# Macaron block on one Trainium2 core: the second feed-forward layer as seven half products, with values and keys staged through DRAM by group and by half

## The reference

```python
def ffn(x):                      # k0: 512 x 1024, k1: 1024 x 1024, k2: 1024 x 256, entries +1 or -1
    h = concatenate([x, -x], axis=-1)
    h = relu(s0 * (h @ k0)) * 2
    h = relu(s1 * (h @ k1)) * 2
    return s2 * (h @ k2)
x = x + 0.5 * ffn(layernorm(x))
x = x + attention(layernorm(x))  # q, k, v projections with biases, softmax, output projection
x = x + 0.5 * ffn(layernorm(x))
```

## Time and profile before

| | us |
|---|---|
| median of 3 runs | 1525.29 |
| span of the profiled execution | 1521.2 |
| TensorE busy | 1512.4 |
| ScalarE busy | 1129.3 |
| VectorE busy | 574.2 |
| GpSimd busy | 59.7 |

### The profile page before, as it was taken

How to read it: one execution, slowest core, us unless ns; L and a number is a source line. 1 busy time by engine, 2 the same in 40 slices (tenths; PEclk the granted TensorE clock), 3 DMA queues, 4 the chain that set the end, 5 groups by cost and what they waited for, 6 DMA issues and landing times.

```text
span 1521.2 us, 31574 instructions
## 1 busy us (share of the span) xinstructions
PE 1512.4 (99%) x12471; PEld 606.1 (40%) x12471; DVE 574.2 (38%) x1298; ACT 1129.3 (74%) x1654; POOL 59.7 (4%) x65
## 2 busy tenths in 40 slices
PE   9999999999999999999999999999999999999999
PEld 5555455334334333333333334334333334334354
DVE  7645764511431243234332333242241332323462
ACT  3221222888889988898989989889988988988721
POOL 2010011001000100010100000000000000000000
PEclk9999999999999999999999999999999999999999
DMA  4122223212331231232223123111213212311110
GB/s 139 42 84 51 75 80 113 71 51 81 84 73 41 96 95 40 67 113 63 81 53 95 40 53 94 39 49 59 81 39 67 82 51 65 104 41 21 47 28 16
DMA packets 110139, 101.46 MB, mean 67 GB/s; under 512 B 55846, under 2 KB 95526, under 8 KB 109990
## 3 DMA queue, kind: packets, MB, share of 16 engines
q1 hardware_dynamic: 109158, 98.60, 23.0%
q10 hardware_dynamic: 832, 0.79, 0.2%
HBM read 61.87 MB, written 25.43 MB: 57 GB/s over the span
## 4 chain that ended last, share of the span: by engine, by line
PE 99%; DVE 0%; ACT 0%; issue 0%; POOL 0%; POOLq 0%
PE psum L888 31%; PE psum L850 30%; PE psum L872 16%; PE psum L750 12%; PE psum L762 3%; PE psum L738 3%; PE psum L769 2%; PE psum L782 1%; PE psum L688 0%; PE psum L775 0%; DVE xn L972 0%; DVE h_lo L982 0%; PE psum L710 0%; DVE x_sb L987 0%; ACT xn L911 0%
## 5 line engine op out<-in xcount | busy, mean ns | idle before, releaser
L942 ACT ACTIVATE prob<-psum 128x512 f32<-128x512 f32 (+1 forms) x1438 | 1016.6, 784 | 120.1 <-PE psum L872 115.4
L888 PE MATMUL psum<-prob,v_sb 128*17 128x512 f32 x4096 | 489.4, 595 | 0.0
L872 PE MATMUL psum<-q_st,k_st 64*128 64x512 f16 x2048 | 350.1, 379 | 0.2
L915 ACT ACTIVATE h_hi<-psum 128x512 f16<-128x512 f32 x183 | 109.6, 604 | 215.8 <-PE psum L750 164.6
L980 DVE TENSOR_SCALAR h_hi<-psum 128x512 f16<-128x512 f32 x73 | 50.5, 692 | 433.8 <-PE psum L850 433.8
L982 DVE SCALAR_TENSOR_TENSOR h_lo<-psum,h_hi 128x512 f16<-128x512 f32 x256 | 169.0, 688 | 86.9 <-ACT h_hi L915 84.4
L888 PEld LDWEIGHTS psum<-prob,v_sb 128*17 128x17 f32 x4096 | 95.3, 96 | 262.9 <-issue 166.4
L872 PEld LDWEIGHTS psum<-q_st,k_st 64*128 64x128 f16 x2048 | 82.5, 94 | 279.1 <-ACT prob L942 210.7
L850 PE MATMUL psum<-h_hi,w 64*128 64x512 f16 x1184 | 152.1, 376 | 0.2 <-ACT h_hi L915 0.2
L850 PE MATMUL psum<-h_lo,w 64*128 64x512 f16 x1184 | 152.0, 376 | 0.0
L750 PE MATMUL psum<-h_hi,w 128*128 128x512 f16 x432 | 102.5, 380 | 2.2 <-DVE h_lo L982 2.2
(11 more groups left out here) (109 smaller groups left out, 860.0 us busy)
## 6 DMA issues: line engine op xcount, KB each, us to landing
k_st<-k_halves SPq DMA_DIRECT2D x64, 512.0 KB, 4.4
q_halves<-piece SPq DMA_DIRECT2D x32, 256.0 KB, 2.5
q_st<-q_halves SPq DMA_DIRECT2D x64, 128.0 KB, 4.8
x_rows<-x_sb SPq DMA_DIRECT2D x16, 256.0 KB, 2.2
k_halves<-piece SPq DMA_DIRECT2D x16, 256.0 KB, 2.8
att_rows<-o_sb SPq DMA_DIRECT2D x128, 32.0 KB
x_sb<-x_rows SPq DMA_DIRECT2D x8, 512.0 KB, 4.0
att_t<-att_rows SPq DMA_DIRECT2D x16, 256.0 KB
```

What stands on the lines that cost most here:

```text
L872: mm = pe.matmul(psum[:, score_bank[h + r], :], k_st[rows, slot, t * P:(t + 1) * P], q_st[rows, slot, :], start=True, stop=True)
L888: mm = pe.matmul(psum[32 * j:32 * j + va, O_BANK, :], v_sb[:, b * key_tiles + t, GROUP * g4 + j, :], prob[:, h % PROBS, :], start=(t == 0) ...
L915: act.activation(hi, psum[:, bank, :], ACT.Relu).then_inc(act_done, 1)
L942: act.activation(prob[:, to:to + count, :], psum[:, bank:bank + count, :], ACT.Exp, scale=score_scale / QK_SCALE ** 2).then_inc(exp_sem, 1)
```

## The change

The second layer of every block but block 0 is computed by Strassen's algorithm in the form with 7 products and shared sums. The 1024 x 1024 weights are cut in 2 x 2 quarters, the activations in 2 x 2 by features and by tokens (256 tokens, `HALF`). Each product is a quarter of the weights, or a sum of quarters, by a quarter of the activations or a sum of them; it is laid in two halves of 256 output features ("p" steps: 14 a block), each 16 matmuls of 128 rows and 256 columns (high and low parts, 4 contraction tiles, 2 output tiles). The two tiles share a bank ahead of and behind attention. Products 2, 7, 4 and 3 go on in the bank of the product before them (`BEFORE`), once that has been read; product 4 adds to 7, which adds to 6.

- **Weights:** `w1` holds the quarters and three sums made by GpSimd; the fourth sum takes the place of a quarter behind block 0's second layer ("w3").
- **Operands:** the first layer's output goes as float32 to `sums` (one buffer, 8 slots, used also for the products). Per pair of tiles VectorE makes T1 to T4, then their high and low parts in float16 (4 x 256 elements); ScalarE, or VectorE in the attention stage, makes the high parts of the three plain quarters and GpSimd their low parts (3 x 256 elements).
- **Outputs:** VectorE adds every product to a sum; products 2, 4, 5 and 3 give a rectified quarter of the result each, high part by ScalarE (VectorE in the attention stage) and low part by VectorE ("low").
- **Order:** "norm" is split in "stat" and "norm"; the normalized rows are GpSimd's but for the first. The first layer of the next block stands ahead of or between the third layer's fills. The attention stage begins with the first layer of block 5. In it a product is one step of 16 slots of 256 columns (two banks, 256 columns of each), a third layer has 13 slots a step for 16, and both rectifications of a first-layer pair are VectorE's.
- **Staging:** values go to DRAM (`v_rows`) by block; for each group values and keys are fetched in two halves of eight key tiles into a single buffer each, in steps 5 and 1 of a group, after the half that they replace has been read. Queries are fetched as before.
- Scaling constants of the first layer are halved (`ACT0_SCALE`).

The core of the diff:

```diff
+A11, A12, A22, S1, S2, S3, S4 = range(7)
+A21 = S3
+B11, B21, B22, T1, T2, T3, T4 = range(7)
+PRODUCTS = {
+    1: (A11, B11, True, None, (1, 0), (0, 1)),
+    2: (A12, B21, False, 0, (2, 0), (0, 2)),
+    6: (S2, T2, True, None, (0, 1), (0, 1)),
+    7: (S3, T3, False, None, (0, 1), (0, 1)),
+    4: (A22, T4, False, 2, (1, 1), (0, 2)),
+    5: (S1, T1, True, 3, (1, 1), (0, 2)),
+    3: (S4, B22, False, 1, (1, 1), (0, 2)),
+}
+FIRST_OF = {1: 1, 2: 1, 6: 6, 7: 6, 4: 6, 5: 5, 3: 5}
+BEFORE = {2: 1, 7: 6, 4: 7, 3: 5}
+OF_QUARTER = {0: 2, 1: 3, 2: 4, 3: 5}
...
-        steps = [Step("norm", u, kind), Step("xn", u, kind)]
+        steps = [Step("stat", u, kind), Step("norm", u, kind), Step("xn", u, kind)]
         if kind == 1 or u:
             steps += [Step("split", u, kind), Step("flip", u, kind)]
         return steps
+
+    def products(u):
+
+        if u <= qblocks or u >= 2 * blocks - 1:
+            order = ((1,), (6,), (2,), (7, -2), (5,), (4, -5), (3, -4, -3))
+        else:
+            order = ((1,), (2, -2), (6,), (7,), (4, -4), (5, -5), (3, -3))
+        return [[Step("p" if k > 0 else "low", u, 8 * half + abs(k)) for k in ks]
+                for half in range(2) for ks in order]
...
+        for i, product in enumerate(second):
+            if i == 3 and ahead is not None and ahead < blocks:
                 steps += norm_turn(0, ahead)
...
+            if early and i == 7:
                 steps += projections(behind)
...
+            if project and i == (11 if last else 9):
                 steps += project + norm_turn(2, ahead)
...
+            if last and i in (0, 2):
+                steps += divide[2 * i:2 * i + tpb]
+            steps += product
+            if not last and i in (2, 5):
+                steps += divide[tpb * (i // 3):tpb * (i // 3 + 1)]
...
+        if ahead is None:
+            steps += third_layer(u)
+        elif last:
+            steps += third_layer(u) + first_layer(ahead)
+        elif u < qblocks:
+            steps += first_layer(ahead, (0, 1)) + third_layer(u, (0,)) + first_layer(ahead, (2,))
+            if behind is None:
+                steps += first_layer(ahead, (3,)) + third_layer(u, (1,))
+            else:
+                steps += third_layer(u, (1,)) + first_layer(ahead, (3,))
+        else:
+            steps += first_layer(ahead) + third_layer(u)
...
-    PAIRS = {"l1": (4, 4), "l2": (5, 3), "l3": (10, 6), "qk": (1, 1), "v": (2, 2), "out": (2, 2)}
...
+    PAIRS = {"l1": (4, 4), "p": (8, 8), "l3": (8, 5), "qk": (1, 1), "v": (2, 2), "out": (2, 2)}
...
+    LONG = {"stat": 0.45, "norm": 0.6, "xn": 0.05, "split": 0.4, "flip": 0.6, "merge": 0.4, "heads": 0.26, "peak": 0.3}
...
+        lay_long(0.6 if side[0].kind == "p" else math.inf)
...
+    while in_group():
+        lay_pair(side[0].n - side[0].hi if side[0].kind == "p" and side[0].n else 16 if side[0].kind == "p" else 64)
+        lay_idle(att_steps)
+        lay_long(math.inf)
...
-        v_sb = sb("v_sb", [P, tokens // P, heads, va], F32)
+        v_new = sb("v_new", [P, block_groups, tpb, GROUP * va], F32)
+        v_st = sb("v_st", [P, key_tiles, GROUP * va], F32)
...
-        w1 = sb("w1", [P, kh, hidden], F16)
+        w1 = sb("w1", [P, 7, kh // 2, hidden // 2], F16)
...
+        h0_hi = sb("h0_hi", [P, 7, kh // 2, HALF], F16)
+        h0_lo = sb("h0_lo", [P, 7, kh // 2, HALF], F16)
...
-        k_st = sb("k_st", [P, 4, seq], F16)
+        k_st = sb("k_st", [P, 2, seq], F16)
+        sums = sb("sums", [P, 8, HALF], F32)
...
+            pool.tensor_tensor(w1[:, S1], w1[:, A21], w1[:, A22], ALU.add).then_inc(w1_sums, 1)
+            pool.wait_ge(w1_sums, 1)
+            pool.tensor_tensor(w1[:, S2], w1[:, S1], w1[:, A11], ALU.subtract).then_inc(w1_sums, 1)
+            pool.wait_ge(w1_sums, 2)
+            pool.tensor_tensor(w1[:, S4], w1[:, A12], w1[:, S2], ALU.subtract).then_inc(w1_sums, 1)
...
+                    if j == 0 and product in BEFORE:
+                        before = find["p", u, 8 * half + BEFORE[product]]
+                        wait_held(before)
+                    if half == 0 and tile == 0:
+                        wait_operand(u, product, low, k)
+                    mm = pe.matmul(psum[:, bank, tile * HALF:(tile + 1) * HALF],
+                                   w1[:, weights, k, (2 * half + tile) * P:(2 * half + tile + 1) * P],
+                                   (h0_hi, h0_lo)[low][:, operand, k, :], start=(starts and j == 0), stop=(j == s.n - 1),
+                                   skip_group_check=True)
...
+                for tile in range(2):
+                    r = (tile + turned) % 2
+                    rows = slice(64 * r, 64 * r + 64)
+                    mm = pe.matmul(psum[:, SHARED[tile], 0:HALF],
+                                   w1[rows, weights, k, (2 * half + tile) * P:(2 * half + tile + 1) * P],
+                                   (h0_hi, h0_lo)[low][rows, operand, k, :], start=(starts and i == 0), stop=(i == s.n - 1),
+                                   skip_group_check=True)
...
+        def sums_free(engine, s):
+
+            u, j = s.u, s.m % 4
+            if j or sums_no[u]:
+                engine.wait_ge(low_b, kh // 2 * sums_no[u] + j)
+            if j:
+                engine.wait_ge(dve_done, find["l1", u, j - 1 + kh // 2].dve)
+            elif sums_no[u]:
+                for product in (2, 5, 4, 3):
+                    engine.wait_ge(dve_done, find["low", sums_of[sums_no[u] - 1], 8 + product].dve)
...
+        def act_first(s):
+
+            u, m = s.u, s.m
+            act.wait_ge(mm_done, s.mm)
+            if m < kh // 2:
+                sums_free(act, s)
+            act.activation(b_rows(sums, m), halves_of(psum[:, s.bank, :]), ACT.Relu).then_inc(act_done, 1)
+            if m >= kh // 2:
+                act.wait_ge(act_done, s.act0 + 1)
+                act.wait_ge(mm_done, last_product(u).mm)
+                act.activation(h0_hi[:, 0:3, m % 4, :], sums[:, 0:3, :], ACT.Copy).then_inc(act_done, 1)
+
...
+            dve.tensor_tensor(sums[:, T1, :], sums[:, T1, :], sums[:, B11, :], ALU.subtract).then_inc(dve_done, 1)
+            dve.wait_ge(dve_done, at + 1)
+            dve.tensor_tensor(sums[:, T2, :], sums[:, B22, :], sums[:, T1, :], ALU.subtract).then_inc(dve_done, 1)
+            dve.wait_ge(dve_done, at + 2)
+            dve.tensor_tensor(sums[:, T3, :], sums[:, T2, :], sums[:, B11, :], ALU.subtract).then_inc(dve_done, 1)
+            dve.tensor_tensor(sums[:, T4, :], sums[:, B21, :], sums[:, T2, :], ALU.subtract).then_inc(dve_done, 1)
+            dve.wait_ge(dve_done, at + 4)
+            dve.wait_ge(mm_done, last_product(u).mm)
+            dve.tensor_copy(h0_hi[:, 3:7, j, :], sums[:, 3:7, :]).then_inc(dve_done, 1)
+            dve.wait_ge(dve_done, at + 5)
+            dve.tensor_tensor(h0_lo[:, 3:7, j, :], sums[:, 3:7, :], h0_hi[:, 3:7, j, :], ALU.subtract).then_inc(dve_done, 1)
+
...
+                dve.tensor_tensor(sum_of(product), both, sum_of(to), ALU.add).then_inc(dve_done, 1)
+            if not s.on_act and PRODUCTS[product][3] is not None:
+                dve.wait_ge(dve_done, s.dve0 + 1)
+                dve.tensor_scalar(second_pair(h1_hi, s.m), sum_of(product), 0.0, None, ALU.max).then_inc(dve_done, 1)
...
+            dve.scalar_tensor_tensor(second_pair(h1_lo, s.m), sum_of(s.m % 8), 0.0, second_pair(h1_hi, s.m),
+                                     ALU.max, ALU.subtract).then_inc(dve_done, 1)
...
-                dve.tensor_scalar(xn[:, place[u, s.m], t, :], x_sb[:, u % RING, t, :], moment[:, n % 2, t, 0:1],
+                engine.tensor_scalar(xn[:, place[u, s.m], t, :], x_sb[:, u % RING, t, :], moment[:, n % 2, t, 0:1],
                                   rstd[:, n % 2, t:t + 1], ALU.subtract, ALU.mult).then_inc(ln_x, 1)
...
+                elif s.kind == "l1" and u and m >= kh // 2 and s.last():
+                    if s.on_act:
+                        pool.wait_ge(act_done, s.act)
+                    else:
+                        pool.wait_ge(dve_done, s.dve0 + 2)
+                    pool.tensor_tensor(h0_lo[:, 0:3, m % 4, :], sums[:, 0:3, :], h0_hi[:, 0:3, m % 4, :], ALU.subtract
+                                       ).then_inc(low_b, 1)
+                elif s.kind == "xn" and norm_no[u, m]:
+                    normed(pool, s)
...
+                    g, step = divmod(s.u, group_steps)
+                    if step == 0 and g + 1 < groups:
+                        sp_stage_q(g + 1)
+                    if step == 1 and g:
+                        sp_stage_keys(g, 1)
+                    if step == group_steps // 2 + 1 and g + 1 < groups:
+                        sp_stage_keys(g + 1, 0)
...
+            if g:
+                sp.wait_ge(qk_sem, 2 * key_tiles * (g - 1) + (half + 1) * key_tiles)
+                sp.wait_ge(pv_sem, key_tiles * (g - 1) + (half + 1) * key_tiles // 2)
...
+                sp.dma_start(k_st[:, pair, at], k_rows.unsqueeze(1).broadcast_to((4 * hd, 2, seq // 2))
```

(4 more changed lines are left out.)

467 lines of the change are left out of this document (340 added, 127 removed).

## The result

The changed kernel takes 1737.85 us (median of 4 runs, 1736.32 to 1739.76) against 1524.8 (1523.85 to 1525.33): ratio 1.14, 95% interval 1.1384 to 1.1416. The forecast was 1664, the top of its range 1698: the direction was right, the time 74 us too short and outside the range. The profiled execution's span is 1735.8 us.

The account below looks back on a forecast made before the run. VectorE's queue, stretched by GpSimd, was to become the bound at every first layer. TensorE's 1467.6 + 32 + 37 + 71 + 42 + 10 = 1660, + 4.1 = 1664 us; range 1548 to 1698.

Parts of the forecast that it names:

- TensorE's own account: Whole kernel: TensorE's own work falls from 1521.2 to 1467.6 us (less 11.4, 14.0, 16.5, 11.7) if no queue falls behind.
- the waits before products 7 and 4: Ahead of attention, blocks 1 to 4: TensorE waits for VectorE's reads behind normalizations, 3.4 and 4.6 us, 32 in all.
- the first layer's waits ahead of attention: First-layer pairs of 6.6 us, single buffer of sums: TensorE waits 12 before block 1, 8.2 in blocks 2 to 4; 37.
- The normalized rows on GpSimd: Each normalization: rows moved from VectorE (1.38 us) to GpSimd, taken as 1.45 us, with VectorE waiting for them.
- the upper bound of 2.4: Normalized rows on GpSimd: at most 4 x 256 x 2.31 ns = 2.4 us, from its two-input rows.
- six gaps: Lower granted clock behind TensorE's gaps, 1.7 us each: one in blocks 1 to 4 each, two behind attention; 10 us.
- Attention's pairs, 71: In attention a first-layer pair takes VectorE 7.28 us in steps of 4.56: TensorE loses 7.1 in each of ten blocks.
- Exclusion: First-layer pairs: GpSimd's subtraction cannot run beside VectorE's two-input sums, so a pair takes 6.6 us, not 4.96; forecast case, 0.62.
- side by side: Rival: VectorE and GpSimd overlap at first-layer pairs, so their waits shrink and the time is 1580 us; chance 0.26.
- The forecast's weighing of the earlier trace: A 64-element VectorE sum took 1.69 us beside GpSimd's 1024-element addition; taken as exclusion, though possibly a one-partition oddity.
- Behind attention, 42: Waits behind attention: product 4 12.7 us behind reciprocals, product 3 7.5, block 15's first layer 18, same-bank products 4.
- Staging: Three more transfers a group on SP's queue, priced at nothing; rival that halves land late: up to 146 more, chance 0.03.

Follow-up runs that it names:

- the extra matmuls: Changed kernel plus 22 matmuls at each of eight waits before products 7 and 4: behind the bank's wait 1751.45 us; ahead of every wait 1733.65 us.
- the memset: Changed kernel with GpSimd's subtraction of 768 elements replaced by a memset to zero, low parts left out: 1665.63 us, ratio 1.0928.

## Why the prediction was right in direction and 74 us short

By stage, the forecast against the span: ahead of attention 225.6 of own work + 69 of waits + 6.8 of clock = 301.4, measured 330.2; attention 1151.7 + 71 = 1222.7, measured 1264.0; behind it 72.1 + 42 + 3.4 = 117.5, measured 123.4. The differences, 28.8 + 41.3 + 5.9, make up the 76 between 1660 and 1735.8. By term, the forecast was too low by 51 for the clock, 18 for TensorE's own account, 18 for the waits before products 7 and 4 and 1 for all other waits, and too high by 12 for the first layer's waits ahead of attention.

**"The normalized rows on GpSimd: [...] I take 1.45, as it is a one-input operation"** failed: 4.83, twice the upper bound of 2.4. The bound was worked out from two-input rows on the belief that one input is cheaper. For an operation with two constants that holds, in a row of the kernel before that the forecast does not show:

```profile
L617 POOL TENSOR_SCALAR wq_sb<-wq_sb 128x512 f32<-128x512 f32 x1 | 0.6, 620 | 0.1
```

That is 1.2 ns an element. The normalized rows take two scalars per partition (mean and reciprocal root) in place of constants and took 1.22 us for 256 elements, 4.8 ns each. No row of the kernel before had this form on GpSimd, so the bound was none. Eight waits before products 7 and 4 sum to 49.9 for 32. The forecast's working with 4.83 in it gives 59, so part of this error was covered by luck: the working overrates these waits. Put back on VectorE the rows give 35.9 us, close to half of the 74, some 11 of it through the clock.

**The clock: "I charge six gaps [...]: 10. In attention the bound is ten more, 17; I take 0"** failed, and this is the largest term. Busy time over the own work is 29.9 ahead of attention and 8.7 behind it, and 22.3 in attention against the same matmuls at 1.00: 61 us. The price of one gap was near (1.7 forecast, 2.3 seen behind a wait of 6.9); the count was not. The changed kernel's trace has 27 stretches at the lower level, 12 ahead of attention (three a block), 12 in it and 3 behind it, 2.3 us each. In attention the waits recur 27 times at the pairs, and the scores between them did not keep the clock up; with the memset, where the waits at the pairs fall from 49.6 to 26.6, two stretches are left there. The 61 are not all time, as the extra matmuls show: ahead of attention part of them lies between two waits for VectorE.

**The first layer's waits ahead of attention** were 24.8 where I had 37: 9.5 before block 1 for 12, and about 5 in each of blocks 2 to 4 for 8.2. A pair takes 6.34 there and not 6.6, which gives 1 us a block; the rest is open. The clock is not the reason: the pairs of block 3 ran at 1.00 (window 175.0 to 218.8).

**TensorE's own account, 1467.6,** was short by about 18 in attention (1169.9 at full clock against 1151.7). 129 product steps took 4.61 and not 4.56, 6.5 us: I took the third layer's step for the product's. (The second layer's old steps, which they replace, took 4.54, as the sum over 256 steps holds them; against these it is 9.8.) 50 third-layer steps took 4.36 and not 4.23, 6.5 us: a change of row halves inside a step, 0.25, that I had not seen in the earlier trace rows, where it falls on the edge. Some 2 to 5 us have no name.

**Attention's pairs, 71:** the mechanism and the pair were right (7.28 forecast, 7.31 measured) by two errors that cancel. The cast of 768 elements takes 0.95 and not 0.58, while GpSimd's subtraction of 1.75 mostly hides behind other sums. The stage's idle time is 71.8, and that this meets 71 is luck too. The waits at the pairs sum to 49.6; a further 12.9 appear at values, because `dve_o` stands in VectorE's queue behind the pair when a group ends there; the rest is small waits. The forecast looked for who waits behind each inserted instruction at the reads of products, and not at this copy.

**Exclusion, against side by side:** decided by the rows (T2's median is 1.75, its minimum 0.42) and by the memset, worth 72 us with the clock's part in it (the forecast had 84 between its two cases). The forecast's weighing of the earlier trace rows was right, and so was the rule of the Trainium skill, SBUF — State Buffer, section Who interferes with whom, that a VectorE instruction with two SBUF inputs contends with a GpSimd instruction that reads SBUF and not with one that only writes it: 0.43 beside the memset, 2.60 beside the addition.

**Behind attention, 42 (45.3 with the end of the last block):** 45.9 of idle time. Product 7's read behind the reciprocals made the wait before product 4 12.8 (forecast 12.7). Product 3's was 11.4 for 7.5, again GpSimd's rows; the first layer's 15.6 for 18.

**Staging:** nothing, as taken.

## What to carry to other kernels

An algorithm that saves matmuls pays on another engine: here 54 us of TensorE's time by the forecast's count (1521.2 to 1467.6), and about 36 by the steps as they came out, were bought with 392 us of VectorE's and 242 of GpSimd's (busy time after less before), and the bill came wherever a read that TensorE needs stood behind that work. Before moving an instruction to GpSimd, price the same form there, operands of scalars included, and ask what reads SBUF beside it; handing 1.6 us of rows a normalization to GpSimd cost 36 us, and taking 0.99 us a pair back from it gained 16. A lower clock behind a wait costs time only if the next wait is not for the same late engine, so fill or shorten the last wait of a run, not the first.

## What the runs showed of the hardware that was not expected

- GpSimd's subtract and multiply with two scalars per partition, 256 float32 elements: 1.22 us (1.216 to 1.584 in 92), 4.8 ns an element. Its additions of two tensors in the kernel before take 2.3, and a multiplication and addition with two constants 1.2 (512 elements in 0.62 us). VectorE does the same rows in 0.41.
- VectorE's cast of three rows of 256 float32 elements to float16 takes 0.95 us, that of four rows 0.69: fewer elements, more time.
- Two matmul streams on the two halves of the rows lose 0.25 us where they change halves inside a step (steps of 4.50 for 4.25 with 13 slots). Steps of 16 slots, with the change on their edge, took 4.56, all 36 of them alike.
- The granted clock was 0.50 over the 3 us behind waits of 2.8 and 6.0 us, and 1.00 behind waits of 1.2 and 1.8. Behind three waits of 3.2 it was 1.00, 0.71 and 0.55.
